# Four graph layers on one core: the softmax multiply of the head stage stands on GpSimd instead of VectorE, with four buffers for exponentials, sums and reciprocals

## The reference, cut to what matters

```
def _L2_gnn_ref(input, adj, W, a_w, a_b):          # H = 8 heads
    h = input @ W
    a1, a2 = (a_w[:, :F], a_w[:, F:])
    s1 = jnp.einsum('bif,hf->bhi', h, a1)
    s2 = jnp.einsum('bjf,hf->bhj', h, a2)
    e = jax.nn.leaky_relu(s1[:, :, :, None] + s2[:, :, None, :] + a_b[None, :, None, None])
    att = jnp.where(adj[:, None, :, :] > 0, e, NEG_INF)
    att = jax.nn.softmax(att, axis=-1)
    h_prime = jnp.einsum('bhij,bjf->bif', att, h) / att.shape[1]
    return h_prime
```

## Time and profile before

| | before |
|---|---|
| median of 3 runs | 2234.93 us (2232.7 to 2235.05) |
| the profiled execution | 2239.13 us, its span 2237.3 us |
| DVE busy | 1892.8 us, 85% of the span |
| PE busy | 1857.5 us, 83% |
| ACT busy | 1568.4 us, 70% |
| POOL busy | 334.0 us, 15% |
| TensorE clock granted, mean of the span | 0.936 |

### The profile page before, as it was taken

How to read it: one execution, slowest core, us unless ns; L and a number is a source line. 1 busy time by engine, 2 the same in 40 slices (tenths; PEclk the granted TensorE clock), 3 DMA queues, 4 the chain that set the end, 5 groups by cost and what they waited for, 6 DMA issues and landing times. The chain is left out here.

```text
span 2237.3 us, 43782 instructions
## 1 busy us (share of the span) xinstructions
PE 1857.5 (83%) x13411; PEld 1155.8 (52%) x13419; DVE 1892.8 (85%) x2726; ACT 1568.4 (70%) x3389; POOL 334.0 (15%) x282
## 2 busy tenths in 40 slices
PE   2978888888867888886799999999999577877886
PEld 2857777777754555665544444444444233333346
DVE  5978888888876999997899999999999466666766
ACT  0634554455436888883499999999999577777773
POOL 1510000000001110103322222222221000000001
PEclk9979999999986999996699999999999799999998
DMA  6000000000000000000155555555555799999982
GB/s 170 0 8 1 1 0 0 0 0 0 0 1 13 6 4 5 5 5 19 49 209 204 216 202 211 206 212 204 212 206 206 268 358 349 345 353 348 353 288 78
DMA packets 122539, 297.25 MB, mean 133 GB/s; under 512 B 20352, under 2 KB 56456, under 8 KB 122264
## 3 DMA queue, kind: packets, MB, share of 16 engines
q1 hardware_dynamic: 105336, 287.69, 34.3%
q10 hardware_dynamic: 16896, 8.39, 1.3%
q0 software_dynamic: 256, 0.56, 0.1%
HBM read 154.78 MB, written 141.82 MB: 133 GB/s over the span
## 5 line engine op out<-in xcount | busy, mean ns | idle before, releaser
L1239 DVE TENSOR_TENSOR v_pairs<-hd 128x2048 f32 (+1 forms) x128 | 291.8, 2280 | 0.0
L1244 DVE TENSOR_TENSOR v_pairs<-hd 128x2048 f32 (+1 forms) x128 | 291.4, 2277 | 0.0
L1300 ACT ACTIVATE v_hid<-v_psW 128x1024 f32<-128x1024 f32 x256 | 265.5, 1037 | 18.1 <-PE v_psW L1341 9.6
L724 DVE TENSOR_REDUCE m_part<-m_psS 128x128 f32<-128x1024 f32 (+1 forms) x192 | 216.9, 1130 | 67.1 <-PE m_psS L603 67.0
L1341 PE MATMUL v_psW<-v_pairs,p_w1T 128*64 128x512 f32 x1024 | 247.5, 600 | 26.8 <-DVE v_pairs L1239 26.8
L1303 ACT ACTIVATE v_junk<-v_psW 128x1024 bf16<-128x1024 f32 x256 | 266.4, 1041 | 0.0
L603 PE MATMUL m_psS<-m_onehot,m_tableT 64*128 64x128 f32 x2816 | 217.3, 293 | 34.2 <-DVE m_part L724 18.0
L1341 PE MATMUL v_psW<-v_pairs,l_w1T 128*64 128x512 f32 (+1 forms) x1024 | 243.2, 587 | 0.0
L956 ACT ACTIVATE a_ex<-a_eu,a_nmx 128x128 f32<-128x128 f32 x512 | 197.8, 390 | 42.2 <-PE a_psA L925 34.3
L1224 POOL COPY v_weights<-p_split 128x192 bf16 (+1 forms) x64 | 154.0, 2407 | 476.9 <-PE v_psW L1341 466.6
L1483 DVE SCALAR_TENSOR_TENSOR s_hid<-s_hid 128x1024 f32<-128x1024 f32 x128 | 155.8, 1221 | 66.6 <-ACT s_hid L1543 66.6
(11 more groups left out here) (251 smaller groups left out, 3573.9 us busy)
## 6 DMA issues: line engine op xcount, KB each, us to landing
pair_hidden<-v_hid SPq DMA_DIRECT2D x256, 512.0 KB, 2.6
s_h<-pair_hidden SPq DMA_DIRECT2D x128, 1024.0 KB, 7.4
s_wide<-pair_scores SPq DMA_DIRECT2D x64, 128.0 KB, 6.0
adj_ring<-in_adj_dram ACTq DMA_DIRECT2D x16, 256.0 KB, 5.0
x_all<-in_x_dram ACTq DMA_DIRECT2D x16, 256.0 KB, 5.3
out_dram<-o_res SPq DMA_DIRECT2D x16, 256.0 KB, 2.3
pair_scores<-s_rot SPq DMA_DIRECT2D x64, 32.0 KB, 6.0
p_ends<-in_c_ends_dram SPq DMA_DIRECT2D x1, 1024.0 KB, 4.7
```

Source lines behind the costliest of these rows:

```text
L724: nc.vector.tensor_reduce(part[:, i, r, :], psS[:, 2 * (at % 2):2 * (at % 2) + 2, 0:w].rearrange("z q (c i) -> z i q c", i=N), AX.XY, ALU. ...
L1239: nc.vector.tensor_tensor(slab(s), one, far, ALU.max).then_inc(max_done, 1)
L1244: nc.vector.tensor_tensor(slab(s), one, far, ALU.subtract).then_inc(sub_done, 1)
L1300: nc.scalar.activation(hid[:, s, :], psW[:, buf, :], ACT.Identity, accum_out=hsum[:, bass.ds(m, 1)]).then_inc(evacuated, 1)
```

## The change

Only `phase_heads` is changed. The multiply leaves DVE's stream and stands in POOL's, in the same slot of the same graph, behind a wait on `recip`. POOL's layer norm of quad g+2, which ran in a loop of its own as soon as its buffer was free, now stands behind the multiply of slot 1 of quad g. `ex`, `zs` and `rz` have four buffers each, and the waits that guard them look four graphs back instead of two. DVE keeps the reciprocal.

```diff
-        ex = sb("ex", [N, 2, HC])
+        ex = sb("ex", [N, G, HC])
...
-        zs = sb("zs", [N, 2, HEADS])
-        rz = sb("rz", [N, 2, HEADS])
+        zs = sb("zs", [N, G, HEADS])
+        rz = sb("rz", [N, G, HEADS])
...
             @block.gpsimd
             def _(pool):
-                def step(g, p):
+                pool.sem_inc(scaled, BIAS)
+
+                def normal(g, p):
                     pool.wait_ge(transposed, done(g - 2))
                     normalize(nc, k, pool, xn[:, p, :], 2, g)
-                with pool.Fori(0, QUADS // 2) as t:
-                    for u in (0, 1):
-                        step(2 * t + u, u)
+
+                def slot(g, p, i, behind, ahead):
+                    n = g * G + i
+                    if behind(3):
+                        at = (i - 3) % G
+                        pool.wait_ge(recip, done(n - 3))
+                        per_head = ex[:, at, :].rearrange("n (h j) -> n h j", j=N)
+                        nc.gpsimd.tensor_tensor(per_head, per_head, rz[:, at, :].unsqueeze(2).broadcast_to([N, HEADS, N]),
+                                                ALU.mult).then_inc(scaled, 1)
+                    if i == 1 and ahead(2):
+                        normal(g + 2, p)
+                normal(0, 0)
+                normal(1, 1)
+                graphs(pool, slot)
...
-                            last = nc.tensor.matmul(psA[:, 0:N], ex[:, (i - 3) % 2, b(h)], k.ident[:, :],
+                            last = nc.tensor.matmul(psA[:, 0:N], ex[:, (i - 3) % G, b(h)], k.ident[:, :],
...
-                        act.wait_ge(att_mm, done(m - 2))
-                        act.wait_ge(recip, done(m - 2))
+                        at = (i - 2) % G
+                        act.wait_ge(att_mm, done(m - G))
+                        act.wait_ge(recip, done(m - G))
...
                         dve.wait_ge(expd, done(m))
-                        dve.wait_ge(scaled, done(m - 2))
-                        nc.vector.reciprocal(rz[:, odd, :], zs[:, odd, :]).then_inc(recip, 1)
-                        dve.wait_ge(recip, done(m))
-                        per_head = ex[:, odd, :].rearrange("n (h j) -> n h j", j=N)
-                        nc.vector.tensor_tensor(per_head, per_head, rz[:, odd, :].unsqueeze(2).broadcast_to([N, HEADS, N]),
-                                                ALU.mult).then_inc(scaled, 1)
+                        at = (i - 3) % G
+                        dve.wait_ge(scaled, done(m - G))
+                        nc.vector.reciprocal(rz[:, at, :], zs[:, at, :]).then_inc(recip, 1)
```

More of the change, by code:

```diff
@@ L952, in slot @@
                         act.wait_ge(negmax, done(m))
-                        act.wait_ge(att_mm, done(m - 2))
-                        act.wait_ge(recip, done(m - 2))
+                        at = (i - 2) % G
+                        act.wait_ge(att_mm, done(m - G))
+                        act.wait_ge(recip, done(m - G))
                         for h in range(HEADS):
-                            last = nc.scalar.activation(ex[:, i % 2, b(h)], eu[:, i % 2, b(h)], ACT.Exp,
-                                                        bias=nmx[:, i % 2, h:h + 1], accum_out=zs[:, i % 2, h:h + 1])
+                            last = nc.scalar.activation(ex[:, at, b(h)], eu[:, i % 2, b(h)], ACT.Exp,
+                                                        bias=nmx[:, i % 2, h:h + 1], accum_out=zs[:, at, h:h + 1])
                         last.then_inc(expd, 1)
@@ L972, in _ @@
             def _(dve):
-                for s in (s_split, leaky, negmax, recip, scaled, att_ready, added):
+                for s in (s_split, leaky, negmax, recip, att_ready, added):
                     dve.sem_inc(s, BIAS)
```

## The result

| | before | after |
|---|---|---|
| median | 2234.99 us of 4 runs (2232.7 to 2235.16) | 2212.96 us of 4 runs (2206.8 to 2214.0) |
| ratio, 95% interval | | 0.9895 (0.9879 to 0.9911) |
| profiled execution | 2239.13 us, span 2237.3 | 2213.4 us, span 2211.6 |
| DVE / POOL busy, whole span | 1892.8 / 334.0 us | 1813.7 / 447.0 us |

What follows compares the result with a forecast made beforehand. DVE was taken to bound the head stage. Gains of 1.04 + 0.21 us a quad made 17.5, plus 1.0 for filling, less 1.3 at the end and 3.3 for the clock: 13.9, median 2221 us, range 2212 to 2229.

Steps and rivals of the forecast that it cites:

- What bounds before: Head stage before the change: DVE sets the pace, 96% busy, 20.77 us a quad; ACT's waits of 33.5 us called largest.
- The new wait: DVE's copy to `attT`: DVE waits some 1.8 us for the sum over heads, twice a quad, leaky relu and maxima queued behind.
- split and finish: DVE's remaining work per quad, about 4.6 us: the split 2.62 behind slot 1's maxima, the finish about 2 behind slot 3's.
- the path: Reciprocal, POOL's multiply, sum over heads, copy to `attT`, leaky relu, maxima: decides the pace, about 19.5 us a quad.
- The path's terms: Steps from reciprocal to maxima: handover to POOL 0.28, multiply 2.08, POOL to PE 0.13, sum over heads 2.05, among others.
- the lower bound of some 2.0: POOL's multiply: lower bound in us if a fixed part of the layer norm's time isn't doubled; 2.08 was taken.
- A turn: One pass from a reciprocal through the maxima, covering two slots: 7.44 us, twice a quad.
- The clock's term: Sum over heads at 1.2 GHz takes 0.94 us more; allowed for in one quad of four, 3.3 us in all.
- the clock falls in every quad: Rival for TensorE's clock in the head stage: 13.2 off 17.2 leaves 4.0 us gain, 2231 us; chance 0.14.
- The end of the stage: End of the head stage: nothing hides the longer multiply, which costs 1.3 us.
- The filling of the pipeline: The quad before the 13, from the moment the pipeline is full: adds about 1.0 us of gain.
- Collisions: DVE's multiply and POOL shutting each other out at SBUF: 0.21 us a quad, which goes with the move.

Runs made afterwards that it cites:

- buffers_only: The changed kernel with the multiply back on DVE and POOL's layer norm in its own loop, four buffers kept: 2233.53 us, ratio 0.9982 to the kernel before.
- delay_02: The changed kernel with one more POOL instruction (0.61 us, result unused) ahead of the multiply in slots 0 and 2 of each quad: 2233.87 us.
- delay_13: The changed kernel with one more POOL instruction (result unused) ahead of the multiply in slots 1 and 3 of each quad: 2213.80 us.
- late_copy: The changed kernel with DVE's copy to `attT` moved behind the leaky relu: 2196.52 us, ratio 0.9840 to the kernel before.
- filled runs: Three unread matmuls added in slot 2: changed kernel 2200.80 us; with the `attT` copy behind the leaky relu 2190.54, plus POOL delay 2204.83; kernel before 2235.81.
- two_buffers: The changed kernel with two buffers of exponentials, sums and reciprocals instead of four, guarded two graphs back: 2218.37 us, ratio 0.9918 to the kernel before.

## Why the prediction was right, and its sizes

*What bounds before* held, though one reading was off: the largest wait of an engine that matters wasn't ACT's 33.5 us but PE's, for DVE's copy to `attT`:

```profile
PE a_psO L913 <- DVE a_attT L1020: 41.2, 34, 1.8
```

It too names DVE. buffers_only shows it best: with ACT's wait for buffers taken away, DVE's 20.5 us a quad stay.

*The new wait* held in place and kind: reciprocals of slots 0 and 2, a wait at the copy twice a quad, the leaky relu behind it, split and finish in full on the path. delay_02 and delay_13 show it to 0.02 us; late_copy shows that the order in DVE's queue was the cause of the wait.

*The path's terms* were too long. The multiply took 1.90, not 2.08: twice the layer norm counted its fixed part twice, and the lower bound of some 2.0 was still above it. With 0.61 us for 256 columns, 1.04 for 512 and 1.90 for 1024, the fixed part is about 0.18 and a column costs 1.67 ns. Reciprocal to multiply was 0.26, not 0.48: the handover from DVE to POOL takes 0.08, so it isn't the receiving engine alone that made 0.28 in the row that I took. POOL to PE was 0.05, not 0.13. A turn is 0.26 + 1.90 + 0.05 + 2.05 + 0.13 + 0.21 + 1.25 + 1.14 = 6.99, not 7.44; two turns with 4.6 for split and finish are 18.6, and the quads without a fall took 18.61. These terms gave 0.9 us a quad, 12.6 in 14, more than forecast. The 1.96 times of "GPSIMD Engine Reference", section 3.1, of the Trainium skill, measured there on 2048 fp32 elements, would have made the multiply 2.4 and doesn't hold here: 1.90 is 1.55 times VectorE's 1.23.

*The clock's term* was too small. I allowed for a fall in one quad of four at 0.94 us. There were falls in 9 of 13 at 1.15, 0.80 a quad in place of 0.24: 7.9 us of gain lost. I had that as a rival, "the clock falls in every quad", with 0.14; what I missed is that the clock of 0.94 before already stood for 9 falls in 13 quads, hidden only from the time. The row was there, and I read it as a share and not as a count. The filled runs show the whole price: 12 us.

*The end of the stage* had the wrong sign: forecast 1.3 lost. From the fifteenth finish row to the next stage's statistics it is 18.28 us before and 15.04 after, 3.2 gained. I priced the longer multiply, but not ACT's last exponentials, which before waited there for a buffer. That stretch takes 15.6 us in buffers_only and 17.5 in two_buffers, so it is the buffers that shorten it.

*The filling of the pipeline* gave 1.7, not 1.0: from the statistics ahead of the stage to the first finish row it is 61.1 us before and 59.4 after. In sum: 13.9 forecast, + 12.6 (path) - 7.9 (clock) + 4.5 (end) + 0.7 = 23.8, against the stage's 24.6.

So the mechanism was right, and that the number came so near is in part luck. The quads of 19.41 us lie between the 19.3 and 19.9 named only because a path that was forecast 0.9 us too long met a clock that cost 0.56 us more a quad than was allowed for. The 8 us between forecast and median are what is left of terms that were off by +12.6, -7.9, +4.5 and +0.7 us in the profiles and partly cancel.

*Collisions* went as forecast: no DVE instruction of the stage is at twice its length, the leaky relu's longest is 1.23, and POOL's multiplies spread over 5 ns. This agrees with "SBUF — State Buffer", "Who interferes with whom", of the Trainium skill, by which a VectorE instruction with at most one SBUF input doesn't contend with GpSimd outside the two-port modes: the leaky relu has one input in PSUM and shares the time with a multiply without loss.

## What to carry to other kernels

When work moves off the engine that sets the pace, follow the product: the engine that gave the work away may stand still at the point where it takes the result back, with its own queue behind it. Put what doesn't depend on the result ahead of that wait; here one instruction moved by one place gave 16 us, and the same move cost 10 us where DVE did the multiply itself and had no wait to fill. And count the falls of TensorE's clock before a change shortens what covers them: removing those hidden under DVE's work gave nothing here, and on the path each cost over 1 us.

## What the runs showed of the hardware

- TensorE's clock fell to 1.2 GHz behind pauses of 1.0 to 1.8 us, mostly that of slot 2 (1.83 us before, 1.33 in the changed kernel, 1.04 with the late copy), for some 3.3 us, once for 7. The same pauses also stand in quads without a fall. With three further matmuls in slot 2 the changed kernel kept 2.4 GHz for 260 us without a break; PE's busy share rose from 90% to 93%.
- POOL's two-input fp32 instructions, each with at least one broadcast input, cost 1.67 ns a column and 0.18 us fixed, in three widths (256, 512 and 1024 columns: 0.612, 1.040 and 1.896 us).
- The handover from DVE's reciprocal to POOL's multiply is 0.08 us from end to start (802.84 to 802.92), that from PE to POOL was 0.28.
